# A vision-text block on one core: quantising the MLP's input in the attention stage, and a new order of the MLP stage with the down product in two pieces

## The reference

```
h   = concat(patches(x) @ W + b, txt)          # 196 + 128 = 324 rows of 256 per image
h1  = h + attention(layernorm(h))              # 16 heads of 16, causal
out = h1 + ffn(layernorm(h1))
ffn(x) = q4(silu(q4(x) @ q4(Wg)) * (q4(x) @ q4(Wu))) @ q4(Wd)     # 256 -> 704 -> 256
q4(v): in blocks of 16, scale = max(max|v| / 6, 1e-12);
       v / scale is rounded to the grid 0, .5, 1, 1.5, 2, 3, 4, 6 (with sign), times scale
```

## Time and profile before

| | us |
|---|---|
| median of 3 runs | 2210.34 (2206.11 to 2213.74) |
| the profiled execution | 2218.46 |
| its span, first to last instruction | 2216.7 |
| busy in it: PE, PEld | 1947.3, 1510.2 |
| DVE, POOL, ACT | 1749.4, 1212.3, 1049.8 |
| granted TensorE clock, mean | 0.94 of full |

### The profile page before, as it was taken

How to read it: one execution, slowest core, us unless ns; L and a number is a source line. 1 busy time by engine, 2 the same in 40 slices (tenths; PEclk the granted TensorE clock), 3 DMA queues, 4 the chain that set the end, 5 groups by cost and what they waited for, 6 DMA issues and landing times. The chain is left out here.

```text
span 2216.7 us, 39676 instructions
## 1 busy us (share of the span) xinstructions
PE 1947.3 (88%) x15200; PEld 1510.2 (68%) x15200; DVE 1749.4 (79%) x3071; ACT 1049.8 (47%) x2075; POOL 1212.3 (55%) x1209
## 2 busy tenths in 40 slices
PE   3899999999999999999999848888888888888888
PEld 3677777777777777777776536666666666666666
DVE  5577676767676777677766349999999999999995
ACT  1355455555545455545554324444444444444443
POOL 5345454544454454545444216666666666666664
PEclk8799999999999999999999659999999999999997
DMA  5464645556465546464635021111111111111100
GB/s 117 69 95 83 94 84 83 94 81 96 75 100 79 91 79 101 77 99 78 103 59 78 14 62 34 36 37 36 36 37 36 41 39 36 36 36 36 36 30 29
DMA packets 129906, 141.94 MB, mean 64 GB/s; under 512 B 19894, under 2 KB 124854, under 8 KB 129718
## 3 DMA queue, kind: packets, MB, share of 16 engines
q1 hardware_dynamic: 122806, 138.40, 35.8%
q10 hardware_dynamic: 6912, 1.00, 0.3%
HBM read 51.25 MB, written 23.40 MB: 34 GB/s over the span
## 5 line engine op out<-in xcount | busy, mean ns | idle before, releaser
L548 DVE TENSOR_REDUCE maxima<-maxp 108x2 f32<-108x648 f32 (+2 forms) x448 | 415.1, 927 | 279.1 <-PE maxp L818 278.7
L727 ACT ACTIVATE probs<-expp 108x648 f32<-108x648 f32 (+2 forms) x512 | 364.3, 711 | 398.0 <-PE expp L843 374.5
L467 POOL TENSOR_SCALAR_AFFINE_SELECT probs<-probs 108x216 f32<-108x216 f32 (+1 forms) x512 | 239.2, 473 | 492.4 <-ACT probs L727 489.9
L1128 POOL TENSOR_TENSOR q_b<-t_b,m_b 128x960 f32<-128x960 f32 (+2 forms) x85 | 192.3, 2263 | 271.9 <-DVE t_b L1190 271.9
L815 PE MATMUL maxp<-kst,qst 96*108 96x108 bf16 (+2 forms) x1536 | 272.6, 271 | 28.4 <-DMA kst<-parts 14.3
L843 PE MATMUL expp<-qst,kst 99*108 99x324 bf16 (+2 forms) x1536 | 241.7, 267 | 33.0 <-DMA qst<-negparts 18.5
L815 PEld LDWEIGHTS maxp<-kst,qst 96*108 96x108 bf16 x1536 | 165.7, 133 | 112.7 <-DVE maxima L548 58.4
L59 PE MATMUL gu<-wgu_hi,xqT 128*128 128x512 f32 (+1 forms) x486 | 216.0, 444 | 6.7 <-ACT xqT L1298 6.7
L864 PE MATMUL attp<-probs,vblk 108*32 108x324 f32 (+2 forms) x3072 | 221.6, 370 | 0.0
L818 PE MATMUL maxp<-mask_qk,identb 108*108 108x108 bf16 (+2 forms) x896 | 219.4, 251 | 0.0
L843 PEld LDWEIGHTS expp<-qst,kst 99*108 99x108 bf16 x1536 | 143.6, 131 | 96.4 <-DMA qst<-negparts 33.4
(11 more groups left out here) (191 smaller groups left out, 5034.5 us busy)
## 6 DMA issues: line engine op xcount, KB each, us to landing
qst<-parts SPq DMA_DIRECT2D x192, 162.0 KB, 5.4
kst<-parts SPq DMA_DIRECT2D x192, 162.0 KB, 7.5
patches<-in_xT SPq DMA_DIRECT2D x32, 588.0 KB, 4.6
h_dram<-h_rows SPq DMA_DIRECT2D x32, 324.0 KB
xt<-h_dram SPq DMA_DIRECT2D x81, 128.0 KB, 2.4
res<-h_dram SPq DMA_DIRECT2D x81, 128.0 KB, 2.1
out_rows<-ot SPq DMA_DIRECT2D x81, 128.0 KB, 2.1
h<-in_txt SPq DMA_DIRECT2D x32, 108.0 KB
```

What stands on the lines that cost most here:

```text
L467: pool.affine_select(out=at, in_=at, compare_op=ALU.is_ge, fill=0.0, base=0, pattern=[[0, nh], [1, CH]], channel_multiplier=-1).then_inc(p ...
L548: dve.tensor_reduce(rowmax[half][:, h:h + nh, c].rearrange("p (a h) -> p a h", a=2), src, AX.X, ALU.max).then_inc(maxp_free, 1)
L727: act.activation(dst, expp[0:CH, 0:banks, 0:per * w], ACT.Exp, scale=SCALE).then_inc(expp_free, 1)
```

## The change

The result is the same up to rounding; both stages change.

**Attention stage.** An image's layernorm before the MLP and the rounding of the result move here: new steps whose names begin with `x2`, three iterations behind the embedding, so that one iteration is added at the end (32 + 4 in all). Per image: three `bn_stats` and three `bn_aggr` on VectorE, the root on GpSimd, three normalising passes on ScalarE, block maxima, two scales, reciprocal and quotient on VectorE, a square on ScalarE (into bfloat16), two passes over 768 columns on VectorE (`x2 t`, `x2 q`), one product on GpSimd (`x2 out`), and a store by SP to `xq_dram`. Normalising the attention's own input moves from VectorE (L637 before) to ScalarE, into the step `xn`, which now stands behind `neg out` and `proj 0`. `STEPS` is written in a new order; `rest`, `last`, `root`, `patches lo`, `h0b` and `neg out` become steps of their own.

**MLP stage.** It reads the rounded x. Layernorm and the rounding of x are gone. h is rounded with ScalarE's square in place of exponent bits and constant; VectorE takes both remaining passes; GpSimd makes one product `hq` with the whole scale, in plain float32. TensorE turns that (2 transposes for x, 6 for h), ScalarE rounds the high part out of PSUM and VectorE takes the low part from PSUM. `gu` has one buffer. h is padded to 768 columns with zeros, so that all down matmuls have 128 rows. The down product is in two pieces: 12 matmuls with the high part, then the turning of the next h, then 6 with the low part. VectorE reads `down` straight from PSUM.

```diff
+STEPS = [
+    ("h0b",), MAX_A[0], ("x2 stats",), ("xnT", 0), ("attend", 1, 0), ("exp", 2, 0), MAX_A[1], ("xnT", 1), ("tok", 1),
...
+    ("exp", 1, 0), ("attend", 0, 0), ("last", 0), ("v", 0), ("exp", 1, 1), MAX_B[4], ("turnback", 0), ("v", 1),
+    MAX_B[5], ("patches",), ("attend", 0, 1), ("w", 6), ("turnback", 1), ("attend", 0, 2), ("last", 1), MAX_B[6],
+    ("patches lo",), ("w", 7), ("exp", 1, 2), ("v", 2), ("xn shift",), ("neg", 1), ("neg out", 1), ("proj", 0),
+    ("xn",), ("exp", 1, 3), ("w", 8), ("proj", 1),
...
+                def x2_products():
...
+                    pool.tensor_tensor(blocks(x2_out[:]), blocks(x2_q), spread(x2_scale[:], CH, NB2),
+                                       ALU.mult).then_inc(x2_out_done, 1)
...
+                        dve.scalar_tensor_tensor(x2_t[:], x2_sq, ADDEND, x2_y, ALU.add,
+                                                 ALU.add).then_inc(x2_t_done, 1)
...
+                def normalise():
+                    act.wait_ge(xshift_done, n + 2)
+                    wait(act, x2_out_done, n - 2)
...
+            for s in range(STEPS_B):
+                t = tile(s, G)
+                if t is not None:
+                    pe.wait_ge(xT_lo_done, t + 1)
+                    wait(pe, h_done, t)
...
+                t = tile(s, DN)
+                if t is not None:
+                    pe.wait_ge(hT_hi_done, t + 1)
+                    wait(pe, out_done, t)
+                    for w in (wd_hi, wd_lo):
+                        for i in range(len(KH)):
+                            ins = pe.matmul(down, hqT_hi[:, i, :], w[:, i, :], start=i == 0 and w is wd_hi, stop=False)
+                    ins.then_inc(down_hi_done, 1)
+                t = tile(s, HT)
+                if t is not None:
+                    pe.wait_ge(hq_done, t + 1)
+                    wait(pe, hT_lo_done, t)
+                    for i in range(len(KH)):
+                        ins = pe.transpose(turn_h[:, i * P:(i + 1) * P], hq[t % 2][:, i * P:(i + 1) * P], ident[:])
+                    ins.then_inc(h_turned, 1)
+                t = tile(s, DN)
+                if t is not None:
+                    pe.wait_ge(hT_lo_done, t + 1)
+                    for i in range(len(KH)):
+                        ins = pe.matmul(down, hqT_lo[:, i, :], wd_hi[:, i, :], start=False, stop=i == len(KH) - 1)
+                    ins.then_inc(down_done, 1)
```

More of the change, by code:

```diff
@@ L167, in active @@
         return k.quantises
-    if kind in ("xnT", "qk", "v", "part 1"):
+    if kind in ("root", "xn shift"):
+        return k.embeds
+    if kind == "patches lo":
+        return k.loads
+    if kind in ("xnT", "qk", "v", "part 1", "rest", "last"):
         return k.qkv
@@ L1001, in phase_b @@
[L1001 to L1008 removed]
+        silu, h, y, t_sum, q = (sb(f"{a}_b", [P, FF]) for a in ("silu", "h", "y", "t", "q"))
```

654 lines of the change are left out of this document (287 added, 367 removed).

## The result

The changed kernel took **2047.95 us** (median of 4 runs, 2044.74 to 2055.56). The kernel before, run beside it, took 2212.04 (2206.11 to 2214.0). The ratio is 0.9267, 95% interval 0.9235 to 0.9299: 7.3% faster, where the prediction said 12% (1940 us, range 1885 to 2010). The direction was right and the size was not: the time lies 38 us above the range. The profiled execution took 2044.74 us with a span of 2042.9.

A forecast was written before the change was run, and what follows sets the result against it. Before the change VectorE bounds the MLP stage and TensorE the attention stage. Attention 1310, 26.2 to the first gate-up, 587 to the last and 22.5 to the end give a 1946 us span; forecast 1940 us, range 1885 to 2010.

The forecast's parts named there:

- +0.5 us per iteration, +16 in all: Attention stage: net lengthening taken for the iterations already there, bounds -1.5 and +3 us per iteration.
- attention stage longer: Rival: attention iterations 2 us or more longer, VectorE's two-input passes waiting for GpSimd; 2002 us at +2.5; chance 0.18.
- the longer waits for `maxp`: Attention stage: sign of the longer-stage rival, together with VectorE's `x2` passes at over 1.5 us.
- The two waits overlap; nothing is added.: Attention stage: ScalarE normalises behind three issues, about 1 us late, overlapping the wait for late query and key copies.
- B's own share: Attention stage, theory from the experiments: ScalarE's three issues of negated maxima hold the normalising, wherever VectorE is.
- the rival in which it stays low throughout: MLP stage: clock stays at its lower level, 14.6 us per tile, 2520 us, slower than before; chance 0.02.
- about 1 us per iteration: Attention stage: gain from the wait for low patches and part of the wait for negated maxima.
- price 0 to 4 us, I take 1.5: Attention stage: last part of query and key taken later, its copies landing at 734.5 to 738.5, wanted at 734.46.
- 7.3 us per tile: MLP stage: TensorE becomes the bound without waiting, in place of 10.70 us per tile; bounds 6.9 and 8.0.
- The claim that one piece would cost 0.8 us per tile: MLP stage: with h turned straight after x, TensorE would wait 0.8 us per tile for `hq`.
- The last chain: End of the attention stage: the added iteration, from statistics to product with nothing beside it, takes 11 us.
- The MLP rival (hand-offs late): MLP stage: `hq` or ScalarE's copy late, 8.3 us per tile, 80 us more, 2020 us; chance 0.14.

The follow-up runs named there:

- run 4: Changed kernel with all `x2` steps doing nothing, order kept, rows h1 stored twice: 2041.02 us.
- run 5: Changed kernel with GpSimd's low part of the patches waiting for VectorE's negated maxima, and the weights' last product moved behind the second residual sum: 1920.18 us.
- run 1: Changed kernel with VectorE's `w_y<-w_y,w_m` moved from beside GpSimd's low part of the patches to behind the first residual sum: 2024.76 us.
- run 9: On top of run 5, SyncE instead of ScalarE issues the three copies of the second half's negated maxima: 1899.87 us.
- run 2: Changed kernel with GpSimd's low part of the patches moved behind the mask of `exp 1,3`: 1970.41 us.
- run 7: Changed kernel with the turning of h straight behind that of x, so the down product is in one piece: 2140.13 us.

## Why the prediction was wrong, and where it was right

**The step that failed** is the sum for the attention stage, "+0.5 us per iteration, +16 in all", with bounds -1.5 and +3. It was +4.6, 143 us. Four things in it were wrong.

1. The block by GpSimd was put at the wrong instructions. The rival "attention stage longer" named the right mechanism, but weighed it for the passes that the change *adds*, found that they fit in VectorE's room, and priced the result at +2.5 us. The added passes are in fact blocked a little (the quotient takes 1.22 us on average and the last pass 1.38, up to 2.17 in single cases, for 0.97) and cost nothing in this order (run 4); the longer waits for `maxp` that the rival named as its sign did not come. What hurt was an old instruction, `w_y<-w_y,w_m`, that the change had only moved, beside a GpSimd instruction that it had moved as well. The order views showed the low part of the patches standing earlier; the prediction never asked what VectorE does at that time. Cost: with run 5, 3.9 us of the 4.6.

2. "1.4 us of passes end at 736.3, about 1 us after TensorE wants them. The two waits overlap; nothing is added." The place was right and the conclusion wrong. TensorE's waits from 600 to 1200 us name none for `kst`, so there was nothing to overlap with: `vblk` had held TensorE up already, and in run 1, without that, the wait for `kst` is there. And the passes were late by 2.65 us and not 1: the issues began 1.8 us ahead of the first maxima before (732.63 and 734.46) and 0.5 us ahead of them after (733.56 and 734.09), because VectorE was late. B's own share, when all is in time, is 0.6 us (run 9).

3. The clock was costed only for the rival in which it stays low throughout. In the iteration shown, the wait of 2.65 us is followed by 7 us at a clock of 0.50 to 0.58. Over the stage work that runs longer is 1.5 us per iteration, a third of the loss, and it is gone in run 5, where the clock is 0.98. In runs 2, 5 and 9, whose waits are at most 1.6 us at this place, the clock is 0.98 to 1.00.

4. The gain of "about 1 us per iteration" was counted in waits of the weight loads, 16.5 and a part of 31.1 us. What the matmuls of the kernel before waited in the same stretch is less:

```profile
PE expp L843 <- DMA qst<-negparts: 17.8, 12, 2.4
PE tokp L59 <- POOL patches_lo L54: 8.8, 18, 0.7
```

Over some 30 iterations that is 0.6 and 0.3 us in each. The second was gained; the first grew to 25.9 us in 26 iterations, 1.0 in each.

The late last part of keys and queries, "price 0 to 4 us, I take 1.5", cost nothing in the change; it shows, at 0.6 to 0.7 us per iteration, where the wait for `vblk` is gone (runs 1, 2 and 5). The maxima's wait, not counted as a gain, went too.

**What was right.** The MLP stage: 7.3 us per tile was predicted, with 6.9 as the lower bound, and 6.87 measured, just at that bound. TensorE is the bound, without gaps, as said. The timeline of one tile on TensorE, from gate-up to gate-up, shows the sum, and GpSimd's beside it the hand-off:

```profile
1707.13 0.39 PE L59 MATMUL gu<-wgu_hi,xqT_hi 128*128 128x512 f32 x1
...
1710.96 0.38 PE L1322 MATMUL turn_x<-ident_b,xq 128*128 128x128 f32 x2
1711.10 0.96 PE L1330 MATMUL down<-wd_hi,hqT_hi 128*128 128x256 f32 x6
1711.89 0.87 PE L1330 MATMUL down<-wd_lo,hqT_hi 128*128 128x256 f32 x6
1712.61 0.81 PE L1337 MATMUL turn_h<-ident_b,hq 128*128 128x128 f32 x6
1713.18 0.96 PE L1343 MATMUL down<-wd_hi,hqT_lo 128*128 128x256 f32 x6
1713.97 0.39 PE L59 MATMUL gu<-wgu_hi,xqT_hi 128*128 128x512 f32 x1
```
```profile
1710.78 1.39 POOL L1189 TENSOR_TENSOR hq<-q_b,scale_b 128x704 f32<-128x704 f32 x1 [5.14 <-DVE q_b L1247]
```

Start to start, gate-up takes 3.83 us (3.94 in the sum), the 18 down matmuls 1.51 + 0.79 = 2.30 (2.2), the eight transposes 0.14 + 0.57 = 0.71 (0.9), and the switches nothing (0.3). `hq` is ready at 1712.17 and its turning begins at 1712.61. The slack is 0.44 us in this tile (0.8 was forecast), and it can be nothing: in 2 of the 73 tiles from 1500 to 2000 us the weight load of the turning waits for `hq`, 0.3 us at most. The claim that one piece would cost 0.8 us per tile came out at 1.01 (run 7). The ends of the stages are these rows, of VectorE, GpSimd and twice TensorE:

```profile
1434.77 0.42 DVE L596 TENSOR_TENSOR h_rows<-linB,h0b 108x256 f32<-108x256 f32 x1
```
```profile
1445.30 1.49 POOL L496 TENSOR_TENSOR x_n<-xn,x_scale 108x768 f32<-108x768 f32 x1 [7.44 <-DVE xn L711]
```
```profile
1471.88 0.80 PE L59 MATMUL gu<-wgu_hi,xqT_hi 128*128 128x512 f32 x1 [0.93 <-DVE xqT_lo L1201]
...
2022.75 0.40 PE L59 MATMUL gu<-wgu_hi,xqT_hi 128*128 128x512 f32 x1
```

The last chain took 1446.8 - 1435.2 = 11.6 us (11), from there to the first gate-up matmul it was 25.1 (26.2), from the first to the last gate-up 550.9 (587), and from there to the end 20.2 (22.5). With 1310 for the attention stage in place of 1446.8, the same pieces give 1906 us of span. So the forecast of 1946 owed some of its nearness to luck: the attention stage was 137 us over and the rest 39 under, mostly because a tile's transposes came out 0.2 us below the sum and the switches 0.3.

The MLP rival (hand-offs late) had its mechanism right and its cause absent here: run 7 is that rival, at 7.88 us per tile against the 8.3 given.

## What to carry to other kernels

When a change moves steps in a hand-written order, list every VectorE instruction that then stands beside a long GpSimd one, the untouched and the tiny ones above all, and ask what is queued behind each: beside GpSimd's low part an instruction with two SBUF inputs took the rest of that instruction's time, whatever its own size (0.18 us became 2.52, 0.28 became 3.03), and instructions with one tensor input were held too (0.16 became 1.38). The time to place is that of the *blocking* instruction: give it a semaphore that lets the urgent chain pass first. And keep DMA issues off the queue of an engine whose next compute step is awaited.
